# Row sums once per pair of heads in four column groups, and one product for both heads in narrow slots

## The reference

```python
latent = einsum('bld,dc->blc', x, Wkv_down)            # 64 wide
k = einsum('blc,chk->blhk', latent, Wk_up); v = einsum('blc,chk->blhk', latent, Wv_up)
attn = einsum('bqhd,bkhd->bhqk', q, k) / sqrt(64)
attn = softmax(where(mask, attn, min), axis=-1)        # causal
y = einsum('bhqk,bkhd->bqhd', attn, v)
return einsum('bqhd,hdo->bqo', y, Wout)
...
logits = xt @ w_router; top1 = argmax(softmax(logits)) # position of each token in its expert's queue,
pos = cumsum(onehot)[arange(T), top1] - 1              # accepted while pos < C = 320
```

## Time and profile before

| | |
|---|---|
| median of 3 runs | 2686.41 us |
| the profiled execution | 2683.09 us |
| its span, first to last instruction | 2681.3 us |
| mean granted TensorE clock | 0.972 |
| TensorE busy | 2494.3 us (93%) |
| GpSimd busy | 1701.7 us (63%) |
| VectorE busy | 1550.2 us (58%) |
| ScalarE busy | 1002.2 us (37%) |

### The profile page before, as it was taken

The page is one execution under the profiler, slowest core; times in us unless marked ns, Lnnn a source line. Parts: engine busy times, 40 slices in busy tenths (PEclk is TensorE's granted clock), DMA queues, the critical chain, the costliest instruction groups (busy, mean ns, idle before and its releaser), DMA issues.

```text
span 2681.3 us, 35897 instructions
## 1 busy us (share of the span) xinstructions
PE 2494.3 (93%) x12072; PEld 1588.2 (59%) x12072; DVE 1550.2 (58%) x4378; ACT 1002.2 (37%) x1496; POOL 1701.7 (63%) x1671
## 2 busy tenths in 40 slices
PE   6999999999999999999999999999999999869996
PEld 4555665556655665566556655566556655646663
DVE  4566556665666566655665566656665665235553
ACT  3344334442444334433444244424443344112222
POOL 1677656865687658766786568656876578414444
PEclk7999999999999999999999999999999999879998
DMA  2121100200020001100110002000200011135441
GB/s 81 56 80 56 37 13 13 68 17 13 17 63 18 13 13 41 43 13 17 27 53 17 9 17 67 17 13 17 60 21 13 13 40 43 44 105 161 153 155 57
DMA packets 97062, 118.91 MB, mean 44 GB/s; under 512 B 12480, under 2 KB 75976, under 8 KB 96880
## 3 DMA queue, kind: packets, MB, share of 16 engines
q1 hardware_dynamic: 89712, 99.98, 13.3%
q0 software_dynamic: 7168, 16.64, 1.7%
HBM read 46.91 MB, written 37.90 MB: 32 GB/s over the span
## 4 chain that ended last, share of the span: by engine, by line
PE 63%; POOL 17%; issue 11%; DVE 5%; ACT 2%; DMA 0%; POOLq 0%; SPq 0%; ACTq 0%; DVEq 0%
PE value_ps L683 14%; POOL sums L464 10%; PE turned_ps L660 8%; PE row_ps L636 7%; PE turned_ps L663 7%; PE misc_ps L584 6%; PE turned_ps L844 5%; PE misc_ps L702 4%; PE misc_ps L693 4%; POOL probs L440 2%; PE value_ps L857 2%; PE misc_ps L857 2%; ACT probs L904 1%; POOL slots_x L497 1%; DVE masked_row L1056 1%
## 5 line engine op out<-in xcount | busy, mean ns | idle before, releaser
L904 ACT ACTIVATE probs<-turned_ps 128x1024 f32<-128x1024 f32 (+3 forms) x768 | 616.8, 811 | 959.6 <-PE turned_ps L663 951.3
L464 POOL TENSOR_TENSOR sums<-sums,probs 128x1024 f32<-128x1024 f32 (+3 forms) x512 | 830.2, 1622 | 23.2 <-ACT probs L904 14.2
L1056 DVE CUSTOM_DVE_ANT_0 masked_row<-row_ps,future 128x384 bf16<-128x384 f32 (+3 forms) x1024 | 464.2, 488 | 407.4 <-PE row_ps L636 406.2
L683 PE MATMUL value_ps<-probs,lat_keys 128*64 128x512 f32 (+3 forms) x3072 | 607.2, 507 | 44.7 <-POOL probs L440 41.3
L660 PE MATMUL turned_ps<-q_hl,lat_hi 128*128 128x512 f32 (+3 forms) x1536 | 569.6, 379 | 1.5 <-ACT fold_v L950 1.5
L663 PE MATMUL turned_ps<-q_max,lat_lo 65*128 65x512 f32 (+3 forms) x1536 | 528.0, 352 | 2.6 <-DMA q_max<-max_rows 2.6
L440 POOL TENSOR_SCALAR_AFFINE_SELECT probs<-probs 128x256 f32<-128x256 f32 x512 | 209.9, 410 | 498.1 <-ACT probs L904 497.4
L636 PE MATMUL row_ps<-lat_hi,q_hl 128*128 128x512 f32 (+3 forms) x1536 | 451.2, 365 | 14.2 <-DVE unit_max L1056 7.6
L460 POOL TENSOR_TENSOR sums<-probs 128x768 f32<-128x768 f32 (+1 forms) x128 | 268.6, 2098 | 229.9 <-ACT probs L904 229.9
L660 PEld LDWEIGHTS turned_ps<-q_hl,lat_hi 128*128 128x128 f32 x1536 | 293.8, 191 | 196.2 <-issue 148.3
L683 PEld LDWEIGHTS value_ps<-probs,lat_keys 128*64 128x64 f32 x3072 | 180.8, 137 | 348.8 <-issue 219.6
(11 more groups left out here) (183 smaller groups left out, 2408.7 us busy)
## 6 DMA issues: line engine op xcount, KB each, us to landing
q_max<-q_hl SPq DMA_DIRECT2D x256, 128.0 KB
slots_x<-zero_rows SPq DMA_DIRECT2D x8, 1290.0 KB, 6.2
ex_x<-slots_x SPq DMA_DIRECT2D x64, 129.0 KB, 3.5
x_in<-in_L_attn_x_bld SPq DMA_DIRECT2D x8, 1024.0 KB, 6.4
layer_out<-x_in SPq DMA_DIRECT2D x8, 1024.0 KB, 4.8
ex_w<-in_L_ffn_w_gate SPq DMA_DIRECT2D x32, 256.0 KB, 2.8
ex_w<-in_L_ffn_w_up SPq DMA_DIRECT2D x32, 256.0 KB, 3.2
ex_w<-in_L_ffn_w_down SPq DMA_DIRECT2D x32, 256.0 KB, 3.8
```

The costliest lines, as they stand in the source:

```text
L464: nc.gpsimd.tensor_tensor(sums[c][:, :, q0:BANK], sums[c][:, :, q0:BANK], now[:, :, q0:BANK], ALU.add).then_inc(added, 1)
L683: mm = nc.tensor.matmul(value_ps[h * LD:(h + 1) * LD, q0:BANK], lat_keys[b % 2][:, j, :], probs[:, n % NPROBS, h, q0:BANK], start=(j == 0) ...
L904: nc.scalar.activation(probs[:, n % NPROBS, :, q0:BANK], turned_ps[n % 2][:, :, q0:BANK], ACT.Exp).then_inc(exp_done, 1)
L1056: nc.vector.tensor_tensor_reduce(masked_row[n % 2][:, 0:width], row_ps[n % 2][:, 0:width], future[:, BANK - width:], scale=-1.0, scalar=-M ...
```

## The change

- `total` is called once per pair, in slot 4 of the next pair. It makes four products with a 128x32 block of ones: head h and half c go to the 32 rows `k = 2h + c`, each in a column group of its own. The sums of the first half need two buffers for that (`half_sums`, three in all).
- VectorE's part is spread over three slots: the 32x32 turn of the one bank (`invert`) stands in slot 5, after the maxima of slot 5, and `invert_rows` for the two halves in slots 6 and 8. It now has two copies of 32x16 in it, which put the reciprocals of half c into the 32 rows beside them, so that they fill the 64 rows of a head.
- GpSimd divides the first half in slot 7 of the next pair and the second half in slot 0 of the pair after that.
- In slots 2, 3, 10 and 11 the queries of both heads fit one bank (2 x 256 or 2 x 128), and the scores of both are one product instead of two, for the high and for the low part.
- The turned maxima of the next pair's first half (`maxT`) move from the start of slot 4 to the end of slot 6. The projections move to slots 9 to 11 of p = 0 and 3, 5, 9, 10, 11 of p = 1 (in the last pair to slots 9 to 11), `x1T`, `logits` and `pos` to p = 2 and slot 7 of p = 3, `q` to slot 7 where p is 0 or 1 (from batch 1 on), the roots to slot 8 of p = 1 and slot 2 of p = 2, and with them VectorE's variance and normalisation.
- Three buffers share space with others (the loaded `wkv2`, `logit` and `work_a`, `zero_rows`).

```diff
+        half_sums = [sb(f"half_sums{i}", [P, 2, BANK], F32, attn) for i in range(3)]
+        sums_of = lambda gp, c: half_sums[2 if c else gp % 2]
...
             if gp + 1 < PAIRS:
                 late[1].append(("q", gp + 1, 1))
-                EARLY[gp, 4] = [("maxT", gp + 1, 0)]
+                late[6].append(("maxT", gp + 1, 0))
             if gp:
-                late[4].append(("sums", gp - 1, 1))
-            late[6].append(("sums", gp, 0))
+                late[4].append(("sums", gp - 1))
             if gp + 2 < PAIRS:
-                late[9 if p == NPAIR - 2 else 8].append(("q", gp + 2, 0))
+                late[9 if p == NPAIR - 2 else 7 if b and p < 2 else 8].append(("q", gp + 2, 0))
...
-        for t, i in zip((1, 2, 3, 5, 7, 8, 9, 10), range(NT)):
+        for t, i in zip((9, 9, 10, 10, 11, 11, 11, 11), range(NT)):
             LATE[PAIRS - 1, t].append(("proj", LAST, i))
...
-                    if gp and t == 0:
+                    if gp >= 2 and t == 0:
+                        divide(gp - 2, 1)
+                    if gp and t == 7:
                         divide(gp - 1, 0)
-                    if gp and t == 6:
+                    if gp == PAIRS - 1 and t == 9:
                         divide(gp - 1, 1)
-                    if b and (p, t) in ((1, 0), (2, 0)):
+                    if b and (p, t) in ((1, 8), (2, 2)):
                         roots(b - 1, p - 1)
...
+                if in_one_bank(t):
+                    nc.tensor.matmul(scores_of(n), lat_hi[b % 2][:, keys], q_hl[gp % 2][:, :, cols], start=True, stop=False)
+                    nc.tensor.matmul(scores_of(n), lat_lo[b % 2][:, keys], q_max[:, c, :, q0:BANK], start=False, stop=True
+                                     ).then_inc(turned_full, 1)
+                    return
...
-            def total(gp, c):
-                use = ("sums", gp, c)
+            def total(gp):
+                use = ("sums", gp)
                 bank = take(use)
-                pe.wait_ge(added, gp * NADD + (HPB if c == 0 else NADD))
+                pe.wait_ge(added, (gp + 1) * NADD)
                 for h in range(2):
-                    mm = nc.tensor.matmul(bank[h * LD:(h + 1) * LD, :], ones_f[:, :], sums[c][:, h, :], start=True, stop=True)
+                    for c in range(2):
+                        k = 2 * h + c
+                        mm = nc.tensor.matmul(bank[k * 32:(k + 1) * 32, :], ones_f[:, :], sums_of(gp, c)[:, h, :],
+                                              start=True, stop=True)
...
+                for h in range(2):
+                    src, dst = (64 * h + 32 * k for k in (c, 1 - c))
+                    nc.vector.tensor_copy(rinv[dst:dst + 32, c, :], rinv[src:src + 32, c, :]).then_inc(inverse_done, 1)
+                dve.wait_ge(inverse_done, 3 * n + 3)
...
                             if use[0] == "sums":
-                                invert_rows(*use[1:])
+                                invert(*use[1:])
+                    if gp and t in (6, 8):
+                        invert_rows(gp - 1, t // 8)
```

More of the change, by code:

```diff
@@ L65, in build_layer @@
     NPROBS = 6
+    VALUES = 2
+    LAG = 0
     NHEADS = NPAIR + 1
@@ L240, in build_layer @@
         EARLY, LATE = {}, {}
+        last_sums = ("sums", PAIRS - 1)
         for gp in range(PAIRS):
@@ L272, in build_layer @@
             if b + 1 < B and p == NPAIR - 1:
-                late[5].append(("keys", b + 1))
+                late[5 + LAG].append(("keys", b + 1))
             for t in range(NSLOT):
@@ L276, in build_layer @@
         LAST = B - 1
-        for t, i in zip((1, 2, 3, 5, 7, 8, 9, 10), range(NT)):
+        for t, i in zip((9, 9, 10, 10, 11, 11, 11, 11), range(NT)):
             LATE[PAIRS - 1, t].append(("proj", LAST, i))
-        ENDING = ([("sums", PAIRS - 1, 1)] + [("rest", LAST, i) for i in range(NT)]
+        ENDING = ([last_sums] + [("rest", LAST, i) for i in range(NT)]
                   + [("x1T", LAST, hf, kd) for hf in range(2) for kd in range(KD)] + [("logits", LAST), ("pos", LAST)])
@@ L666, in values @@
             def values(n0):
-                for n in (n0, n0 + 1):
+                for n in range(n0, n0 + VALUES):
                     gp, t = divmod(n, NSLOT)
@@ L809, in _ @@
                         row_scores(*unit)
-                    if t % 2 == 0 and gp + t:
-                        values(gp * NSLOT + t - 2)
+                    if t % VALUES == LAG and gp * NSLOT + t >= VALUES:
+                        values(gp * NSLOT + t - LAG - VALUES)
                     for use in LATE[gp, t]:
                         STAGES[use[0]](*use[1:])
-            values(PAIRS * NSLOT - 2)
+            values(PAIRS * NSLOT - VALUES)
             for use in ENDING:
@@ L1071, in copy_max, with invert @@
                 nc.vector.tensor_copy(max_rows[c][:, :], bank[0:NT, 0:P]).then_inc(misc_free, 1)
-            def invert(gp, c):
-                use = ("sums", gp, c)
+            def invert(gp):
+                use = ("sums", gp)
                 bank = wait_full(dve, use)
@@ L1142, in choose @@
                 use = ("logits", b)
+                if b == 0:
+                    dve.wait_ge(zeroed, 16 * NPAIR)
                 bank = wait_full(dve, use)
@@ L1226, in _ @@
                             if use[0] == "sums":
-                                invert_rows(*use[1:])
+                                invert(*use[1:])
+                    if gp and t in (6, 8):
+                        invert_rows(gp - 1, t // 8)
                     for use in LATE[gp, t]:
-                        if use[0] in STAGES and use[0] != "q":
+                        if use[0] in STAGES and use[0] not in ("q", "sums"):
                             STAGES[use[0]](*use[1:])
-                    if b and (p, t) in ((0, 11), (1, 8)):
-                        variance(b - 1, p)
-                    if b and (p, t) in ((1, 3), (2, 2)):
+                    if b and (p, t) in ((1, 5), (2, 0)):
+                        variance(b - 1, p - 1)
+                    if b and (p, t) in ((1, 10), (2, 4)):
                         normalise(b - 1, p - 1)
@@ L1238, in _ @@
                 if use[0] == "sums":
-                    invert_rows(*use[1:])
+                    for c in range(2):
+                        invert_rows(PAIRS - 1, c)
                 if use[0] == "rest" and use[2] == HPB - 1:
```

76 lines of the change are left out of this document (39 added, 37 removed).

## The result

The changed kernel takes 2668.17 us, median of five runs (2666.28 to 2674.16), against 2686.41 us in the same session: ratio 0.9931, interval 0.9914 to 0.9947. It is faster, by 18 us (0.7%), where 61 were forecast. The direction was right; the time lies inside the wide range and outside the forecast's own one (2605 to 2650). The profiled execution took 2668.64 us.

A forecast was written before the change was run, and what follows sets the result against it. The prediction took TensorE's own order of work, 93% busy, as the bound. Its terms, -26 + 10 - 45 - 16 - 8 - 22 + 39 + 2 + 4, gave -62 us and 2625 us; own range 2605 to 2650, whole range 2584 to 2686.

The forecast's parts named there:

- the four copies: VectorE's copies of 16 columns for the inverses: each below 0.25 us, hidden by its free 42%, so no cost counted.
- the stall in slot 5: TensorE waits for VectorE's later turn of the sums in p = 1, 2, 6, 7: 28 x 1.39 = 39 us added.
- The sums: Row sums called once per pair, in slot 4 instead of slots 4 and 6: 0.70 us per pair, 45 us gained.
- B: Rival: column groups of the row sums run two at a time, 0.88 us more per call; 2681 us, chance 0.13.
- C: Rival: row-sum products start strictly in program order, five steps instead of two; 2709 us, chance 0.10.
- The 0.16 for one more change of the array's division: Row sums in slot 4: an extra switch of TensorE's array tiling with its drain, 0.16 us, between nothing and 0.25.
- The narrow slots: One score product for both heads: 0.20 us gained in slots 3 and 11, 26 us, of which 10 given back.
- The roots: GpSimd's roots moved to slots 8 (p = 1) and 2 (p = 2): TensorE's waits shrink, 22 us gained over seven batches.
- The turned maxima and the bank behind the placing: Slot 4: waits for VectorE's maxima go, 16 us; the sums' wait for the bank behind the placing goes, 8 us.
- `pos` in slot 7: Placing of the tokens moved in p = 3: part of the 8 us gained on the sums' bank wait; no cost counted.
- Rival A: The stall in slot 5 costs nothing, since GpSimd gains time and later waits shrink; 2586 us, chance 0.14.
- Rival D: TensorE doesn't get its shorter slots; GpSimd takes the place of the waits removed; 2668 us, chance 0.15.

The follow-up runs named there:

- e1_recip: The changed kernel with each inverse written to both places by reciprocals from the turned sums, so no copies are left: 2650.18 us, ratio 0.9875.
- e4_both: The changed kernel with reciprocals instead of copies and VectorE's turn of the sums back in slot 4: 2594.0 us, ratio 0.9666.
- e5_roots: The version with reciprocals and the turn in slot 4, with the roots of p = 2 moved to slot 4, normalisation to slot 5: 2600.72 us.
- e10_place: The changed kernel with the placing of the tokens back in slot 3 of p = 3, its exponentials in slot 1: 2663.15 us, ratio 0.9928.

## Why the prediction was right in direction and wrong in size

**The step that failed** is the cost of the four copies: "four copies of 16 columns, unseen before, each surely below the 0.25 of the reciprocal; its free 42% hide that". They took 0.78 us on average and up to 2.32, because a copy begun beside an addition of GpSimd ends only after it. They stand ahead of readers that empty banks, and so TensorE waited: 20.6 us in slot 7 of p = 1, 2 and 6 and 8.1 us in slot 8 of p = 6, both gone in `e1_recip`. VectorE's free 42% hid nothing of that, since what counts is how late it comes to the next bank. "Unseen" asked for a bound from both sides, and I gave one from above without a reason. The trace of the kernel before had rows that should have warned me, scalings within SBUF of four and of eight columns:

```profile
L1128 DVE TENSOR_SCALAR var_eps<-mean_var 128x4 f32<-128x4 f32 x16 | 15.8, 984 | 0.5
...
L1179 DVE TENSOR_SCALAR rt<-rt 128x8 f32<-128x8 f32 x8 | 1.3, 158 | 0.0
```

The smaller one took six times as long (0.17 us at the median, 2.03 at the most). The Trainium skill, SBUF — State Buffer, section Who interferes with whom, states the rule: a copy, a cast or a `tensor_scalar` within SBUF can take the port pair that VectorE shares with GpSimd, and the one that comes second is blocked for the whole instruction. The 0.17 us at most of the copies begun with GpSimd idle and the 2.10 of one begun beside an addition agree with it; the seven copies that took 0.17 us beside a power of 1.04 don't. The reciprocal isn't in its list and wasn't held. By the rule the price to take was what is left of GpSimd's addition, up to 2.4 us, twice a pair, and the question should have been how late VectorE becomes for the banks behind.

**The account.** `e4_both` is the change without the stall in slot 5 and without the copies. The prediction has 2625 - 39 = 2586 us for that; measured are 2594, 92 us below the kernel before. So the sum of everything but these two was right within 8 us, though its terms were not. The two together cost 74 us where 39 was counted for the stall and nothing for the copies: 35 of the missing 43. Undone first, the copies are worth 18 us and the stall 29; undone second, 46 and 56. At one clock that is 31 and 39 first, 35 and 43 second. The other 8:

- The sums: 0.86 us a pair goes and 0.03 comes, 53 us instead of 45. All four groups run together; rivals B and C fall with the 0.99 us. With C falls its reading of the rule that stood beside it, the Trainium skill's, TensorE: Matmul & The Clock Gate, Part 3, What overlaps and what doesn't: that a group waits for the second of the two instructions of the group before. The rule itself, that matmuls start and end in program order, isn't refuted, neither by the 0.96 us, as the prediction had it, nor by the 0.99: four products are under way together within 0.10 us, and they may still have started in order. The 0.16 for one more change of the array's division was not seen.
- The narrow slots: 11 us instead of 16. The two products take 0.35 us, not 0.30, since the first takes 0.22; that makes 128 x 0.15 = 19 us, of which 8 are given back (10 forecast).
- The roots: 1.6 us of p = 1 went as forecast; in p = 2 the wait is 1.87 us for 2.1, where 0.6 was to stay, so 13 us instead of 22. `e5_roots` shows that a later slot doesn't give it back.
- The turned maxima and the bank behind the placing: 15.3 and 7.2 us of idle time gone, as forecast. What wasn't forecast is the 20.6 us that the bank waits behind the same maxima in their new place; it is part of the copies' price. Of the 12.0 us that the row scores wait for VectorE's maxima 7.0 stand in slots 8 and 9 of p = 3, behind the placing; without the copies 11.4 are left.
- `pos` in slot 7, to which the prediction gives a gain and no price: 5 us in the changed kernel (`e10_place`), 15 with the other waits gone (nothing and 10 at one clock). `e4_both` still has it in slot 7, so its price belongs to the 8.

Of these, -8, +5 and +9 make 6, and with 10 for `pos` 16, where 8 are missing. What gives the rest back the runs don't isolate.

**The stall in slot 5** was right in place, kind and size: 1.12 us of idle time (1.2 or more was asked for) at each of 28 places, the release by VectorE's turn, and 29 us gone with it (39 at one clock; 39 forecast). Rival A fell. Rival D gave 2668 us, the measured time to the microsecond, and was wrong: the narrow slots do gain, and the values' waits for GpSimd did not grow. TensorE's busy share did fall, but the waits that were added are waits for VectorE; it is GpSimd that took the gain, through VectorE's copies. A rival that hits the number is not shown by that.

## What to carry to other kernels

Before a small copy, cast or scaling within SBUF goes onto VectorE, look at what GpSimd does there: beside an addition of 2.4 us it cost up to 2.3 us here, though it takes 0.16 by itself; a reciprocal did the same work without being held. Where the change adds an operation unseen in the trace, price it by its longest relative in the trace, not by its size. And before you read a meeting of two costs out of times that don't add up, compare idle time and clock: undone together the two were worth 74 us and apart 47, but their idle time adds up (62 us against 30 and 34), and it was the mean clock that was lower in the single versions.

## What the runs showed of the hardware

- A copy of 32x16 within SBUF: 161 ns free, 781 on average, 2322 at most. Of 256, the 133 that were held began beside a GpSimd instruction and ended 0.02 to 0.04 us after it; seven beside a power of 1.04 us weren't held. A reciprocal of the same size: 230 to 252 ns. A scaling of 128x8: 158 ns or 1806; one of 128x256: 0.41 us at the median, 2.45 beside an addition.
- Four column groups of 32 run together: eight products of 512 columns in 0.99 us, four on two groups in 0.96, sixteen in 1.85.
- After a wait of 1.87 us TensorE's clock was at 0.50, where the eight products of the sums take 1.87 us instead of 0.99, and kernels with less idle time had at times more of it: `e1_recip` ran at 0.960 and the changed kernel at 0.969. I can't say from these runs which wait brings it on.
